# A fused window-attention, linear-attention and routed-expert kernel: zero-padded contraction rows in place of filler matmuls, own PSUM banks for the last expert steps, grouped scatters, and a new order of all steps

## Chip, cores and metric

The kernel runs on one core of a Trainium2 chip. The metric is the device time of one execution in microseconds. The engines are named as in the profile: PE (TensorE), PEld (its weight loads), DVE (VectorE), ACT (ScalarE), POOL (GpSimd), SP (SyncE, which issues DMAs).

## The reference, cut to what matters

The input is 32 images of 56x56 tokens with 64 channels. Three layers follow one another on every token:

```
# layer 0: shifted 7x7 windows, 8 heads of 8, relative position bias, mask; then an MLP with a norm inside
y = ln(x); win = windows(roll(y, -3)); q, k, v = win @ qkv_w.T + qkv_b
x = x + unroll(softmax(q*s @ k.T + bias + mask) @ v @ proj_w.T + proj_b)
h = ln(gelu(ln(x) @ fc1_w.T + fc1_b)); x = x + h @ fc2_w.T + fc2_b
# layer 1a: linear attention over an image, 16 heads of 4
t = ln(x); q, k, v = split(t @ W_qkv.T + b_qkv); kv = einsum(ln(k), ln(v)) / HW
x = x + gelu((q @ kv + t) @ W_proj.T + b_proj) + t
# layer 1b: 8 experts, the best two of each token, weighted by the renormalised softmax
xn = ln(x); x = x + sum_top2(weight_e * (gelu(expert_ln_e(x) @ W1[e] + b1[e]) @ W2[e] + b2[e]))
```

## The kernel before, in words

**Groups and steps.** The tokens are cut into 256 groups of 4 tiles of 98 tokens (two 7x7 windows); an image has 8 groups. Each engine runs a loop over `n`, and in each pass it performs once every short step of the list `ORDER[engine]`. A step's suffix is the group it works on relative to `n`: `s0:+2` computes the scores of group n+2, `fc2:+0` the second MLP matmul of group n, `lp:-10` the linear attention's projection of group n-10 (it needs the sums of the whole image), `rk:-11` the ranks of its tokens among 28 pairs of experts. The order was written out by hand or by a planner; at run time nothing but semaphores ties the engines together. `now`, `before` and `whole` are the waits; `images` runs the list, in steady state from a loop.

**Experts.** Every token is put, by an indirect DMA of POOL, into a queue in DRAM for its pair of experts (`scatter`, four per group). SP reads full tiles of 128 tokens of one pair back (`load_tiles`). There are 271 expert steps of 3 such tiles; step m runs at n = m+26: transposes (`tx`), first matmuls (`ei0` to `ei2`, 8 fp16 matmuls each), gelu on ACT (`h00` to `h23`), second matmuls (`eo0` to `eo2`), weighting on DVE (`yv`, `ya`, `ys`), and three indirect stores of POOL (`so0` to `so2`). A step thus has three tiles, 12 gelus and three stores. Since the groups end at n = 256 and the expert steps at n = 296, the last 40 or so steps run with little or nothing beside them.

**PSUM.** Eight banks: pA serves eight steps of a group in turn (zT, q, z2T, fc11, uT, hT1, oT, proj), pB seven, pO, pP and pS the attention, pK the linear attention, pH the experts' first matmuls, pY both their transposes and their second matmuls. Who may take a bank next is written out in `HANDED`; `handed_on` turns that into a wait.

**Filler matmuls.** `keep_warm` (line 611) issues two fp16 matmuls of 128 rows, 128 columns and 512 moving columns, whose result nobody reads. The PE's list holds eight such steps (fY0, fH0, fS0 to fS2, fB0, fA0, fK0), all at offset -26: they run in every pass that has an expert step, 16 matmuls a pass, and in none of the first 26 passes.

**Contraction rows.** Where a bias is added inside a matmul, the operands have 65 rows: 64 channels and a row of ones (zt, ot, z2t, ut_img, utc on one side, wa, wq2, wp, wf1, wkv, m65 on the other). The router's operands xnt and wrt have 64. `rank` (its first matmul, line 788) and `expert_out` (line 830) contract over a single row, onesf against count or b2pair.

**POOL.** `scatter` waits before each of a group's four DMAs until the one before has landed, `store` likewise before each of its three.

## Time and profile before

| | us |
|---|---|
| median of 3 runs | 9902.23 |
| lowest, highest | 9801.24, 10075.31 |
| the profiled execution, device time | 9946.41 |
| its span, first to last instruction | 9944.6 |
| mean granted TensorE clock in it | 0.821 |

The profile is one execution. Busy time counts an engine's own instructions; idle time in front of an instruction is put down to what released it. A granted clock of 1.00 is 2.4 GHz throughout a stretch, 0.50 is 1.2 GHz throughout. "x" is a count of instructions; an fp32 matmul of the program stands as two matmul instructions. "128*98" in front of a shape are the rows (contraction) and columns that a matmul uses of the array, then comes the moving operand.

### The profile page before, as it was taken

To read this page: it belongs to the slowest core of one execution; us is meant where nothing else is said; L and a number is where in the kernel's file an instruction comes from. 1 tells how busy PE (TensorE), PEld (TensorE's weight loads), DVE (VectorE), ACT (ScalarE), POOL (GpSimd) and SP (SyncE) were. 2 spreads that over 40 slices of the span, in tenths; PEclk is the share of its full clock that TensorE was granted. 3 is DMA by queue.
4 is the path that set the end of the run, shared out by engine and by line. 5 is a ranking of instruction groups with operands and counts; after the bars stand their busy time and mean duration, and the time that the engine had idled before them with its cause. 6 is when DMAs were issued, how large, how long until landed. Compare 5 with 4: busy or idle time off the path is not lost. (4 is left out here: it accounts for less than half of the span.)

```text
span 9944.6 us, 258863 instructions
## 1 busy us (share of the span) xinstructions
PE 9346.8 (94%) x66105; PEld 7341.6 (74%) x66105; DVE 6489.6 (65%) x26878; ACT 5811.1 (58%) x12712; POOL 5304.0 (53%) x7260
## 2 busy tenths in 40 slices
PE   6999999999999999999999999999999999998777
PEld 5777777777777777777777777777777777776544
DVE  4566676577787867677667767677777778673100
ACT  2444566566776756667556656666666667662111
POOL 1344555466665645566555655566665666564311
PEclk8555787699998968899778978899998999886666
DMA  0000000000000000000000000000000000000000
GB/s 22 4 9 9 16 20 17 16 21 21 21 22 20 22 17 19 19 20 21 18 18 19 21 18 19 18 21 20 21 21 19 20 20 22 19 18 21 21 15 9
DMA packets 222232, 181.52 MB, mean 18 GB/s; under 512 B 63338, under 2 KB 193332, under 8 KB 220553
## 3 DMA queue, kind: packets, MB, share of 16 engines
q1 hardware_dynamic: 161128, 84.94, 3.6%
q0 software_dynamic: 59680, 79.82, 2.8%
q8 instruction: 623, 10.21, 0.5%
q14 instruction: 801, 6.55, 0.3%
HBM read 84.61 MB, written 81.62 MB: 17 GB/s over the span
## 5 line engine op out<-in xcount | busy, mean ns | idle before, releaser
L1365 POOL TENSOR_TENSOR sc<-sc,mx 98x392 f32<-98x392 f32 x1024 | 901.6, 881 | 1561.2 <-DVE mx L1013 1495.0
L1606 ACT ACTIVATE ht<-ps,be 128x128 f32<-128x128 f32 x3252 | 1025.2, 364 | 1117.5 <-PE ps L821 534.2
L1428 POOL DMA_INDIRECT slots<-rec,slot x1024 | 1078.3, 1053 | 832.2 <-issue 651.3
L616 PE MATMUL ps<-we_hi,identh 128*128 128x512 f16 x4336 | 1493.1, 448 | 7.7 <-issue 7.3
L1455 POOL DMA_INDIRECT out_y<-ys,row_at x813 | 844.2, 1038 | 738.0 <-issue 297.9
L835 PE MATMUL ps<-we,ht 128*128 x6504 | 1113.3, 326 | 0.0
L835 PEld LDWEIGHTS ps<-we,ht 128*128 128x128 f32 x6504 | 988.6, 233 | 123.7 <-issue 55.0
L651 PE MATMUL ps<-kexp,qbd 128*98 128x392 f32 x2048 | 1028.0, 588 | 5.8 <-DVE sc L1007 3.0
L1007 DVE TENSOR_TENSOR sc<-ps,bias 98x392 f32<-98x392 f32 x1024 | 565.8, 553 | 707.9 <-PE ps L651 676.3
L670 PEld LDWEIGHTS ps<-vexp,pt 98*98 98x98 f32 x8192 | 912.3, 185 | 130.0 <-issue 72.3
L670 PE MATMUL ps<-vexp,pt 98*98 98x36 f32 x8192 | 928.5, 263 | 8.9 <-ACT kexp L1496 8.9
L821 PE MATMUL ps<-xs,we_hi 128*128 128x128 f16 x3252 | 612.7, 240 | 304.1 <-issue 302.0
L1354 POOL TENSOR_TENSOR rs<-ve,cs 98x4 f32<-98x4 f32 x768 | 801.7, 1044 | 20.1
L1481 ACT ACTIVATE pt<-ps 98x392 f32<-98x392 f32 x1024 | 511.8, 500 | 398.9 <-PE ps L670 377.3
L1350 POOL TENSOR_TENSOR ve<-mv,cs 98x4 f32<-98x4 f32 x768 | 218.7, 285 | 940.8 <-DVE mv L967 937.6
L1496 ACT ACTIVATE kexp<-ps,cs 128x196 f32<-128x196 f32 x2048 | 676.7, 462 | 21.2 <-PE ps L635 21.1
L821 PEld LDWEIGHTS ps<-xs,we_hi 128*128 x3252 | 340.8, 105 | 466.4 <-issue 388.8
L659 PEld LDWEIGHTS ps<-cs,pr 98*98 98x98 f32 x4096 | 493.7, 147 | 252.6 <-issue 167.8
L659 PE MATMUL ps<-cs,pr 98*98 98x98 f32 x4096 | 610.5, 279 | 2.4 <-ACT pr L1520 1.7
L616 PEld LDWEIGHTS ps<-we_hi,identh 128*128 128x128 f16 x4336 | 433.9, 117 | 239.4 <-issue 171.2
L821 PE MATMUL ps<-xs,we_lo 128*128 128x128 f16 x3252 | 602.4, 237 | 0.7
L1305 DVE TENSOR_TENSOR yv<-ps,rt 128x384 f32<-128x384 f32 x271 | 149.7, 552 | 682.0 <-PE ps L835 676.8
(233 smaller groups left out, 22351.8 us busy)
## 6 DMA issues: line engine op xcount, KB each, us to landing
rt<-slots SPq DMA_DIRECT2D x813, 66.0 KB
xg<-in_x SPq DMA_DIRECT2D x256, 98.0 KB
slots<-rec,slot POOLq DMA_INDIRECT x1024
out_y<-ys,row_at POOLq DMA_INDIRECT x813
lw<-tile_list SPq DMA_DIRECT2D x271, 0.0 KB
bias<-in_rel SPq DMA_DIRECT2D x1, 1200.5 KB
bias<-in_w SPq DMA_DIRECT2D x2, 512.0 KB
tile_list<-entry SPq DMA_DIRECT2D x64, 0.5 KB
```

Of the source, the lines that this page charges most:

```text
L616: pe.matmul(bank[:, :], identh[:, :], we1[0][:, 0:512], start=True, stop=True)
L651: pe.matmul(pS[0:TOK, 0:HEADS * WA], qbd[:, t, :], kexp[:, t, :], start=True, stop=True)\
L659: last = pe.transpose(pP[0:TOK, cols(h)], pr[:, t, TOK * h:TOK * (h + 1)], ident[0:TOK, 0:TOK])
L670: last = pe.matmul(o[:, :, 2 * h:2 * h + 2, :], pt[:, t % 2, h, :], vexp[:, 2 * t:2 * t + 2, 2 * h:2 * h + 2, :], start=True, stop=True)
L821: last = pe.matmul(pH[:, 128 * (2 * e + h):128 * (2 * e + h + 1)], we1[half][:, bass.ds(pair[e] * HID + 128 * h, 128)], xs[:, q, :], start ...
L835: last = pe.matmul(dst, ht[:, q, 2 * e + h, :], we2[:, bass.ds(chosen[q][e] * 2 + h, 1), :].rearrange("p a c -> p (a c)"), start=False, st ...
L1354: pool.tensor_tensor(rs[L][:, :, :], ve[L][:, :, :], k("minushalf")[0:TOK].unsqueeze(1).to_broadcast([TOK, ve[L].shape[1], GT]), ALU.pow)\
L1365: pool.tensor_tensor(s, s, mx[:, t, :].unsqueeze(2).to_broadcast([TOK, HEADS, WA]), ALU.subtract)\
L1428: pool.indirect_dma_start(slots, bass.IndirectOffsetOnAxis(ap=slot[:, j % 2, t:t + 1], axis=0), rec[:, bass.ts(j % RB, 1), t, :].rearrange ...
L1455: pool.indirect_dma_start(out, bass.IndirectOffsetOnAxis(ap=row_at[:, q:q + 1], axis=0), ys[:, bass.ts(j % 2, 1), q, :].rearrange("p a c - ...
L1496: last = act.activation(kexp[:, :, WA * h:WA * (h + 1)], keys_, ACT.Copy, scale=k("headmask")[:, h:h + 1])
L1606: act.activation(ht[:, q, b, :], pH[:, 128 * b:128 * (b + 1)], ACT.Gelu, bias=be1[:, bass.ds(chosen[q][b // 2] * 2 + b % 2, 1)], scale=1.0 ...
```

## The change

1. **Padded operand rows.** All the 64- and 65-row operands become 128-row ones with zeros below, as do onesf and b2pair; wrt, wa, wp, wf1 and wkv come padded from the host, with the bias row already in them. Four small loads go, nine memsets on DVE in the setup come.
2. **No filler matmuls.** The eight `f..` steps are gone from the PE's list.
3. **Free banks for the last steps.** From expert step 233 (`FIRST_LATE = TOTAL - 23`) on, the transposes go to pA, the first matmuls of the three tiles to pH, pO and pP, the second ones to pY and pS in turn. `groups_done` waits once until the groups are through with these banks.
4. **Scatters and stores in a group.** The waits between the four scatters of a group, and between the three stores of a step, go; one wait for the whole group before stays.
5. **Another order.** All five lists are new but SP's: on PE zT moves from +2 at the head to +3 near the end, v to +1, on DVE st2, mv2, c2 and z2 to +1 and qbd to +3, on ACT sd behind the experts' gelus and just ahead of exp, on POOL the order of sc, so and pw steps.

```diff
-        ut_img = sb("ut_img", [C + 1, TILES * TOK])
+        ut_img = sb("ut_img", [128, TILES * TOK])
...
-        wf1 = sb("wf1", [C + 1, HID])
+        wf1 = sb("wf1", [128, HID])
...
-        load(wf1[0:C, :], fc1w)
-        load(wf1[row, :], fc1b)
+        load(wf1[:, :], fc1w)
...
-            pe="""mix0:+0 fY0:-26 zT:+2 lp:-10 tx:-26 pT0:+1 q:+2 k:+2 fH0:-26 fS0:-26 rk:-11 ei0:-26 mix1:+0 fS1:-26
-                  pT1:+1 fS2:-26 z2T:+0 o0:+1 s0:+2 pT2:+1 o1:+1 fc10:+0 fc11:+0 mix2:+0 ei1:-26 fB0:-26 pT3:+1 xnT:-10
-                  s1:+2 o2:+1 mix3:+0 uT:-1 o3:+1 logit:-10 s2:+2 kv:-1 ei2:-26 mix4:+0 eo0:-26 hT0:+0 hT1:+0 eo1:-26
-                  s3:+2 v:+2 eo2:-26 fA0:-26 oT:+1 fK0:-26 G:-1 proj:+1 fc2:+0""",
...
+            pe="""mix0:+0 lp:-10 k:+2 q:+2 v:+1 rk:-11 tx:-26 z2T:+0 s0:+2 ei0:-26 mix1:+0 pT0:+1 fc10:+0 pT1:+1 mix2:+0
+                  o0:+1 fc11:+0 o1:+1 s1:+2 xnT:-10 uT:-1 mix3:+0 pT2:+1 ei1:-26 logit:-10 pT3:+1 s2:+2 o2:+1 o3:+1 hT0:+0
+                  kv:-1 hT1:+0 ei2:-26 mix4:+0 s3:+2 eo0:-26 oT:+1 fc2:+0 proj:+1 eo1:-26 G:-1 zT:+3 eo2:-26""",
...
+        FIRST_LATE = TOTAL - 23
...
+        def x_bank(m):
+            return pAh if late(m) else pYh
+        def h_bank(m, q):
+            return (pH, pO, pP)[q] if late(m) else pH
+        def y_bank(m):
+            return (pY, pS)[m % 2] if late(m) else pY
...
+            def groups_done():
...
+                if not alone:
+                    alone.append(True)
+                    for signal in ("x1_ready", "hnT_ready", "uT_kept", "o_joined", "pT_ready", "score_bias"):
+                        whole(pe, signal, TOTAL - 1)
...
-                pe.matmul(pB[:, 0:(GT + 1) * NP], onesf[:, :], count[0:1, :].unsqueeze(1).to_broadcast([1, GT + 1, NP]),
+                pe.matmul(pB[:, 0:(GT + 1) * NP], onesf[:, :], count[:, :].unsqueeze(1).to_broadcast([128, GT + 1, NP]),
                           start=True, stop=False)
...
+                if late(m):
+                    groups_done()
+                    if m > FIRST_LATE:
+                        now(pe, "xs_ready", m - 1)
+                else:
+                    handed_on(pe, "tx")
...
-                handed_on(pe, f"ei{q}")
+                if not late(m):
+                    handed_on(pe, f"ei{q}")
+                elif m > FIRST_LATE:
+                    now(pe, "h_ready", m - 1, 4 * q + 3)
...
+            for padded in (zt_, ot, z2t_, ut_img, utc, m65, xnt):
+                dve.memset(padded[C:128], 0.0)
+            dve.memset(onesf[:, :], 0.0)
+            dve.memset(b2pair_[:, :], 0.0)
...
                     whole(pool, "tiles_loaded", g - SCATTER_TO_LOAD - 1)
-                now(pool, "rec_scattered", g, 16 * t - 1, alone="pool")
+                    whole(pool, "rec_scattered", g - 1, alone="pool")
...
-                now(pool, "ys_ready", m)
-                now(pool, "row_ready", m)
-                now(pool, "y_stored", m, 16 * q - 1, alone="pool")
+                if q == 0:
+                    whole(pool, "y_stored", m - 1)
+                    now(pool, "ys_ready", m)
+                    now(pool, "row_ready", m)
+                    pool.sem_inc(held["pool"], 1)
```

## Rows read from the trace of the kernel before

**Rows 1.** The page: the span, and busy time of each engine.
```profile
span 9944.6 us, 258863 instructions
PE 9346.8 (94%) x66105; PEld 7341.6 (74%) x66105; DVE 6489.6 (65%) x26878; ACT 5811.1 (58%) x12712; POOL 5304.0 (53%) x7260
```

**Rows 2.** Busy time by stretch: start, routing, steady, its end, tail, full-speed, half-speed.
```profile
core 0: us, PE busy (x) PEld busy (x) DVE busy (x) ACT busy (x) POOL busy (x), PEclk, DMA share, GB/s
101.00:511.00 410.00, 377.55 (x1823) 299.70 (x1821) 199.91 (x754) 190.32 (x357) 122.96 (x169) 0.60 0.01 4
511.00:1070.00 559.00, 520.88 (x2692) 428.56 (x2690) 353.30 (x1508) 265.50 (x522) 250.29 (x356) 0.55 0.04 9
1070.00:8967.00 7897.00, 7642.45 (x57898) 6062.56 (x57897) 5745.51 (x23867) 5159.39 (x11208) 4669.31 (x6401) 0.87 0.08 19
8967.00:9077.00 110.00, 97.37 (x491) 71.72 (x489) 46.18 (x221) 32.02 (x88) 50.98 (x69) 0.63 0.08 20
9077.00:9944.00 867.00, 666.90 (x2957) 443.62 (x2954) 97.91 (x403) 159.19 (x529) 208.69 (x259) 0.64 0.07 16
2535.00:2781.00 246.00, 234.58 (x2016) 187.06 (x2015) 202.65 (x829) 178.50 (x391) 162.80 (x223) 1.00 0.09 22
1329.00:1375.00 46.00, 46.00 (x220) 36.17 (x220) 23.68 (x102) 20.96 (x44) 19.19 (x26) 0.50 0.05 13
```

**Rows 3.** The same for the experts' transposes (line 802) alone, three to a step.
```profile
1070.00:8967.00 7897.00, 86.33 (x689) 64.92 (x690) 0.87 0.08 19
2535.00:2781.00 246.00, 2.66 (x24) 1.94 (x24) 1.00 0.09 22
```

**Rows 4.** DVE's groups in 9077 to 9908 us: one weighting for each step.
```profile
L1305 DVE TENSOR_TENSOR yv<-ps,rt 128x384 f32<-128x384 f32 x37 | 20.7, 558 | 644.8 <-PE ps L835 644.8
```

**Rows 5.** PE's groups in 2535 to 2781 us: busy, mean ns, idle before.
```profile
L616 PE MATMUL ps<-we_hi,identh 128*128 128x512 f16 x126 | 36.5, 380 | 0.0
...
L696 PE MATMUL ps<-wf,z2t 65*98 65x256 f32 x64 | 15.6, 386 | 0.1
L715 PE MATMUL ps<-wf,hnt 128*98 128x64 f32 x128 | 12.4, 250 | 0.0
...
L684 PE MATMUL ps<-wp,ot 65*98 65x64 f32 x64 | 6.8, 250 | 0.0
...
L635 PE MATMUL ps<-zt,wa 65*64 65x196 f32 x28 | 3.5, 328 | 0.0
```

**Rows 6.** A stretch of the start, 200 to 500 us: all engines, then PE's largest groups.
```profile
200.00:500.00 300.00, 281.92 (x1361) 226.19 (x1359) 152.30 (x579) 143.03 (x271) 92.87 (x130) 0.52 0.01 4
...
L651 PE MATMUL ps<-kexp,qbd 128*98 128x392 f32 x72 | 56.1, 883 | 0.0
...
L696 PE MATMUL ps<-wf,z2t 65*98 65x256 f32 x72 | 33.4, 646 | 0.0
...
L715 PE MATMUL ps<-wf,hnt 128*98 128x64 f32 x129 | 23.4, 374 | 0.0
```

**Rows 7.** PE's timeline around one full-speed filler pair (start us, us).
```profile
2605.13 0.59 PE L616 MATMUL ps<-we_hi,identh 128*128 128x512 f16 x2
2605.56 0.50 PE L659 MATMUL ps<-cs,pr 98*98 98x98 f32 x4
```

**Rows 8.** Waits in 2535 to 2781 us: total us, times, longest.
```profile
POOL sc L1365 <- DVE mx L1013: 26.4, 19, 2.3
...
DVE sc L1007 <- PE ps L651: 9.6, 10, 1.7
```

**Rows 9.** Busy time by stretch for the scores (line 651) alone, eight a group.
```profile
511.00:1070.00 559.00, 88.33 (x120) 25.12 (x120) 0.55 0.04 9
```

**Rows 10.** DVE's timeline in the setup.
```profile
34.01 2.67 DVE L877 MEMSET ut_img<- 1x3136 f32 x1 [0.60 <-issue]
...
48.79 3.15 DVE L931 MEMSET b2pair<- 1x3712 f32 x1 [0.71 <-issue]
```

**Rows 11.** PE's timeline over a step of the tail (start us, us).
```profile
9504.17 0.78 PE L830 MATMUL ps<-b2pair,onesf 1*128 x2
...
9506.78 0.79 PE L830 MATMUL ps<-b2pair,onesf 1*128 x2
...
9514.44 0.53 PE L802 MATMUL ps<-identh,rt 128*128 128x128 f16 x3
...
9516.58 0.24 PE L821 MATMUL ps<-xs,we_hi 128*128 128x128 f16 x1
...
9520.66 0.23 PE L821 MATMUL ps<-xs,we_hi 128*128 128x128 f16 x1 [2.12 <-issue]
```

**Rows 12.** POOL's timeline in the tail: a store behind the one before.
```profile
9517.81 0.98 POOL L1455 DMA_INDIRECT out_y<-ys,row_at  x1 [2.13 <-DMA out_y<-ys,row_at]
```

More of the change, by code:

```diff
@@ L230, in build @@
         pA, pO, pP, pS, pB, pH, pK, pY = ps
-        pYh = pY.ap().bitcast(F16)
+        pYh, pAh = (bank.ap().bitcast(F16) for bank in (pY, pA))
         rec16 = rec.ap().bitcast(F16)
@@ L468, in runs_at @@
                 return n + at == TOTAL
+            if name[0] == "f" and name[1].isupper():
+                return n in range(STEPS + 26)
             if name == "tl":
@@ L605, in transposes @@
                 last.then_inc(S[signal], 1)
-            def keep_warm(name, bank):
-                handed_on(pe, name)
+            alone = []
+            def groups_done():
[3 more added lines that the diff above has]
+                        whole(pe, signal, TOTAL - 1)
+                    pe.wait_ge(mix_dve, 5 * IMAGES)
+                    pe.sem_inc(held["pe"], 1)
+            def keep_warm(name, bank):
+                if late(ran["n"] - 26 if isinstance(ran["n"], int) else None):
+                    groups_done()
+                    bank = pK
+                else:
+                    handed_on(pe, name)
                 for _ in range(2):
@@ L779, in logits @@
                 for t in range(GT):
-                    last = pe.matmul(pB[0:TOK, NE * t:NE * (t + 1)], xnt[0:C, cols(t)], wrt[:, :], start=True, stop=True)
+                    last = pe.matmul(pB[0:TOK, NE * t:NE * (t + 1)], xnt[:, cols(t)], wrt[:, :], start=True, stop=True)
                 last.then_inc(S["logit_psum"], 1)
@@ L1634, in layout @@
     line = lambda a: a.reshape(1, -1)
+    under = lambda w, *b: np.concatenate([w, *b, np.zeros((128 - w.shape[0] - len(b), w.shape[1]), w.dtype)], 0)
     halves = lambda a: a.reshape(2, 128, -1).transpose(1, 0, 2)
```

130 lines of the change are left out of this document (63 added, 67 removed).

## The prediction

> **What bounds the kernel now.** The page comes first. PE is busy 94% of the span, the next engine, DVE, 65% [rows 1]. That is an average over stages, so the second view is the busy time by stretch [rows 2]. In the steady stretch, 1070 to 8967 us, PE is busy 97% and nothing else passes 73%: PE bounds it. It holds 689 transposes, three to an expert step, so 229 steps [rows 3], and a step takes 7897/229 = 34.5 us. In this table the reader is to see the granted clock: 0.87 on average, though PE is hardly ever idle. Two stretches inside it show its levels. In 2535 to 2781 us the clock is 1.00 and eight steps (24 transposes) take 246 us, 30.75 us each. In 1329 to 1375 us it is 0.50, and 220 matmuls take 46 us; at full speed a step has 2016/8 = 252 of them, so a half-speed step takes about 46 x 252/220 = 52.7 us. The 34.5 us lies between: 3.7 us of each step are lost to the clock.
>
> Before 1070 us there are neither experts nor fillers; PE is busy 92 to 94% there and the clock is only 0.60 and 0.55 [rows 2]. After 9077 us only expert steps are left: 37 of them [rows 4] in the 831 us up to the last one's start, 22.5 us each, PE busy 77%, the rest waits for single banks.
>
> The third view is PE's groups at full speed [rows 5]. The fillers (line 616) are its costliest group. Ten other groups have operands of 1, 64 or 65 rows (lines 627, 635, 643, 684, 696, 728, 767, 780, 788, 830), from 15.6 us for line 696 down to 3.5 for line 635.
>
> **The clock, and what padding does to it.** In 200 to 500 us PE is busy 94%, and the clock is 0.52 [rows 6]. In 2535 to 2781 us it is busy 95%, and the clock is 1.00. So being busy doesn't decide. What differs is what PE does: the early stretch has no fillers and no experts, so of its groups only lines 651 and 715 use 128 rows, and everything else has 98 or fewer. I read this as: matmuls that use few rows of the array count for less with whatever grants the clock. Then padding to 128 rows and the fillers are two ways to the same end. Of the matmul time of a full-speed step, the padded groups hold about as much as two times the fillers' (the ten groups sum to 80 us of the stretch, the fillers to 36.5), and it goes from half the array or less to all of it; what is taken away was full. I therefore expect the clock to be at least as high as before.
>
> The Trainium skill has another rule. "TensorE: Matmul & The Clock Gate", Part 1, says that the gate follows how busy the PE has been, and names no rows. By that rule padding is worth nothing and taking the fillers away can only lower the clock; by the trace it is incomplete, since a PE at 94% had 0.52. It would put all the weight on the slower rival below.
>
> Padding itself costs no PE time: line 684 with 65 rows and line 715 with 128 rows, both with 64 moving columns, take 250 ns each [rows 5].
>
> **The change part by part.**
>
> *Fillers.* A pair at full speed starts at 2605.13 and the next group at 2605.56 [rows 7], so 0.215 us each, 16 a step: 3.4 us. PE's work in a full-speed step falls from 234.58/8 = 29.3 to 25.9 us. Now the cover ends: DVE has 202.65/8 = 25.3 us of work in the same step, POOL 20.4 plus the idle issue time in front of its seven indirect DMAs, ACT 22.3 [rows 2]. So PE and DVE are level, and the step can't go below about 26 us. It can't go above the 30.75 us that it has now at full speed unless the new order is worse. At present PE is idle 30.75-29.3 = 1.4 us of a step while DVE has 5.4 us of slack; with no slack left on DVE every wait such as DVE's for scores, 1.2 us a step, and POOL's for maxima, 3.3 us a step [rows 8], hits PE sooner. I take 28.2 us, the middle of 26 and 30.75, because nothing in the rows places it nearer to an end.
>
> *Padding.* The 3.7 us a step lost to the clock stand for a share at half speed of 26% (mean 0.87). I estimate that a fifth of that share is left, since after padding some short stretches of 98-row matmuls and waits remain: 0.6 us. Bounds: 0 and 3.7. Step: 28.8 us; 229 steps: 6595 us.
>
> *Start.* In 200 to 500 us there are 72/8 = 9 groups' scores, a step of 33.3 us [rows 6], so in 101 to 511 some 12 steps; in 511 to 1070 there are 120/8 = 15 of 37.3 us [rows 9]. They are PE-bound at half speed; DVE's work is 200/12 = 17 and 353/15 = 24 us. With full clock they would follow DVE, 20 and 26 us with its gaps; without any gain they stay. These steps lack the experts' 128-row matmuls, so I expect the clock to move up and down and take 26 and 29 us: 410 becomes 320, 559 becomes 435.
>
> *New memsets.* ut_img's took 2.67 us and b2pair's 3.15 [rows 10], both for one partition; the same over 64 or 128 partitions is as long, and the others add about half as much again. That is 9 us in front of everything, on the path: the 101 us ahead of the first stretch become 110. The four loads fewer are taken at nothing, as the wait for the large ones stays.
>
> *Free banks in the tail.* Today the step's transposes start at 9514.44, the first expert matmul at 9516.58, 2.1 us later; the second tile's at 9520.66, held up by the gelus that empty the only bank [rows 11]. A tile's 8 matmuls take 0.95 us, and about 1.0 us of PE's sequencer work lies in front of each tile. With own banks the three tiles end 2.1 + 0.95 + 2 x 1.95 = 7.0 us after the transposes. The second matmuls start every 2.61 us (9504.17 to 9506.78), at half speed, so three take 7.9 us. No fillers between: 15 us. At full clock the latter would be half as long: 11 us. Other limits lie lower: POOL's three stores without a wait take 3 x 1.05 and one landing of 2.1 us [rows 12]. I keep 15, since weight loads and gaps leave the array idle for much of such a step; the range is 11 to 22. 37 x 15 = 555 us. The four steps between 8967 and 9077 still carry the groups' last parts: 110 becomes 96. The stretch behind the last transposes, 36 us, loses two of the stores' waits: 32.
>
> *Scatters in a group.* In steady state POOL isn't the bound and its waits for landings are small; worth nothing there while POOL has its 10 us of slack, which shrinks to 8 at 28.8 us. Without that cover a landing wait of 2.1 us [rows 12] for three of the four scatters would count, 6 us a step, so this edit protects the gain rather than makes one.
>
> *Order.* One activation table load fewer on ACT by the list (sd now stands next to exp), not on the path. The rest of the reordering is what lets PE and DVE come near their 26 us, or doesn't: it is in the 28.2.
>
> **Sum** against the span of 9944.6 us: 110 + 320 + 435 + 6595 + 96 + 555 + 32 = 8143 us. The device time lies 2 us above the span: 8145. The profiled execution is 0.4% above the median of the runs shown; that is within the spread, and I leave 8145.
>
> **Rivals.**
>
> A. *Another engine or the chain takes the place of the fillers.* The fillers stood partly where PE would have waited anyway, so the step stays near its present full-speed length, 31.2 us with a little loss of clock. For it: DVE needs 25.3 us and POOL waits 3.3 us a step for it. Against: PE waits only 1.4 us now. 229 x (31.2-28.8) = 550 us more: 8695. Chance 0.25.
>
> B. *The zeros don't count, slower.* If the clock follows what is multiplied and not how many rows are enabled, or busy time alone, the steady steps look like the start: clock 0.55, nine tenths of the time at half speed. A half-speed step without fillers is 52.7 less 16 fillers at twice 0.215, so 45.8 us, a full-speed one 28.2; mixed: 1/(0.9/45.8 + 0.1/28.2) = 43 us, 9850 us for 229, start as now, 11,600 in all. It decides where a steady step passes (9902-1548)/229 = 36.5 us, which is a share at half speed of 0.6 or a mean clock of 0.70. For it: nothing in the trace has zero rows below an operand. Against: the fillers' own stationary operand is an identity, nearly all zeros, and the transposes' likewise, and stretches full of them are at 1.00. Chance 0.08.
>
> C. *DVE and PE mesh perfectly*, 26.8 us a step: 7687. Chance 0.07. Two engines at 95% or more with semaphores between them speak against it.
>
> D. *Clock and step as forecast*: 0.60; its own range is 7850 to 8450, from 27.5 to 30.1 us a step.
>
> **How the numbers follow.** The likeliest is D: 8145. To hold eight in ten the range takes in D and most of A: 7800 to 8720. It leaves out B, most of C and A's upper end. About 2% is what a measurement of this kernel can tell from no change, as its runs spread by 2.7%. Faster by more than 2%: D, A and C, 0.92. Within 2%: a partial B, 0.02. Slower: 0.06.
>
> **What the profile after would show.** The steady stretch at a clock of 0.93 or more (step "padding"); PE busy about 90% and DVE about 88% there (step "fillers"): if DVE is under 80% and PE has waits of 3 us a step, it is rival A. The start's clock above 0.7. Tail steps of 15 us, first matmuls of the second tile 2 us behind those of the first. The first stretch begins about 9 us later. I am wrong in the main thing if the steady clock is under 0.8, or if the step is under 26 us, which would mean that DVE's busy time itself depends on what runs beside it.

## The result, and the profile after

The changed kernel takes 8790.39 us (median of four runs, 8773.87 to 8800.38). The kernel before took 9988.77 us on the same chip; the ratio is 0.892 with a 95% interval of 0.884 to 0.900. It is faster by over 2%, as forecast, but 645 us slower than the predicted 8145 and 70 us outside the range.

The page of the kernel after: span, and busy time of each engine, beside [rows 1].

```profile
span 8794.7 us, 246765 instructions
...
PE 7712.4 (88%) x61769; PEld 6474.0 (74%) x61769; DVE 6559.0 (75%) x26887; ACT 5510.5 (63%) x12487; POOL 5335.8 (61%) x7260
```

Busy time by stretch of the kernel after, in the columns of [rows 2]: start, routing, steady, its end, tail.

```profile
110.00:422.00 312.00, 257.24 (x1828) 199.25 (x1829) 208.87 (x769) 194.31 (x363) 122.97 (x172) 0.88 0.02 5
422.00:854.00 432.00, 386.51 (x2696) 317.88 (x2695) 355.99 (x1507) 271.42 (x525) 253.73 (x358) 0.75 0.05 12
854.00:8110.00 7256.00, 6521.76 (x54221) 5489.33 (x54220) 5796.40 (x23865) 4845.60 (x10973) 4701.02 (x6399) 0.91 0.08 21
8110.00:8208.00 98.00, 70.71 (x430) 61.08 (x427) 43.97 (x210) 35.11 (x89) 48.30 (x66) 0.57 0.09 22
8208.00:8768.00 560.00, 422.99 (x2292) 362.35 (x2290) 94.75 (x393) 155.47 (x514) 200.74 (x252) 0.50 0.10 25
```

Term by term, predicted and measured: 110 and 110 us ahead of the first stretch, 320 and 312, 435 and 432, **6595 and 7256**, 96 and 98, 555 and 560, 32 and 27. The whole miss, 652 us of span, is in the steady stretch (661). Its 229 steps take 31.69 us each instead of 28.8.

Two parts of that can be told apart. I call a step plain if it isn't the last of an image's eight. In the few plain steps whose granted clock was 1.00 throughout (some 20 of them), the median is 29.76 us: the predicted 28.2 was 1.5 short. The other 1.93 us are lost to the clock; I had 0.6. Those 1.9 us are of two kinds: a plain step dips once, and the last of an image's eight steps takes 38.6 us at a mean clock of 0.74, against means of 29.2 to 31.5 us for the other seven.

Where PE stands idle is in the waits of the kernel after, 2500 to 7000 us, which hold 142 steps (who waited on what; us in total, times, longest):

```profile
POOL sc L1401 <- DVE mx L1049: 750.4, 228, 7.1
...
PE ps L850 <- issue: 195.3, 264, 2.6
...
PE ps L670 <- ACT kexp L1537: 148.0, 115, 1.5
...
PE ps L703 <- ACT ot L1522: 61.0, 124, 0.8
```

These three waits of PE are 1.4, 1.0 and 0.4 us a step (the second is 1.16 with what stands under "issue" there); with the small ones PE is idle 3.2 us of each step. POOL's long wait for DVE costs nothing: DVE itself is busy only 5796/7256 = 80%. PE's timeline shows one of each, three instructions of one step (start us, us, idle before):

```profile
5193.52 0.90 PE L670 MATMUL ps<-kexp,qbd 128*98 128x392 f32 x2 [1.29 <-ACT kexp L1537]
...
5208.72 0.23 PE L850 MATMUL ps<-xs,we_hi 128*128 128x128 f16 x1 [0.93 <-issue]
...
5214.01 0.88 PE L703 MATMUL ps<-wp,ot 128*98 128x64 f32 x8 [0.49 <-ACT ot L1522]
```

"issue" says that nothing the profile knows was waited for. This is line 850, the experts' first matmuls, where PE also loads an entry of the list and works out addresses; e8, e11 and e15 below show that this is what the time goes to. PE's groups of the kernel after in the same stretch (busy us, mean ns, idle before):

```profile
L670 PE MATMUL ps<-kexp,qbd 128*98 128x392 f32 x1136 | 506.8, 528 | 165.2 <-ACT kexp L1537 148.0 <-issue 15.4
...
L850 PE MATMUL ps<-xs,we_hi 128*128 128x128 f16 x1704 | 384.3, 234 | 199.6 <-issue 195.3
L850 PE MATMUL ps<-xs,we_lo 128*128 128x128 f16 x1704 | 374.9, 225 | 0.9
```

The same matmuls in the kernel before, line 821 there, at full speed in 2535 to 2781 us (eight steps):

```profile
L821 PE MATMUL ps<-xs,we_hi 128*128 128x128 f16 x96 | 16.2, 222 | 5.7 <-issue 5.7
...
L821 PE MATMUL ps<-xs,we_lo 128*128 128x128 f16 x96 | 15.8, 218 | 0.1
```

Each matmul is nearly as long as before, at a lower clock, but the idle time in front has doubled, from 0.7 to 1.4 us a step.

### The profile page after: what moved, and what is told of

The parts are those of the page before. It is cut to its first block and busy times, and to the rows that moved or that the text cites. A ratio compares the mean times of both kernels' runs of the same rounds, so it can differ in the third digit from the quotient of the medians.

```text
span 8794.7 us, 246765 instructions
## 1 busy us (share of the span) xinstructions
PE 7712.4 (88%) x61769; PEld 6474.0 (74%) x61769; DVE 6559.0 (75%) x26887; ACT 5510.5 (63%) x12487; POOL 5335.8 (61%) x7260
## 5 line engine op out<-in xcount | busy, mean ns | idle before, releaser
L670 PE MATMUL ps<-kexp,qbd 128*98 128x392 f32 x2048 | 929.1, 536 | 270.9 <-ACT kexp L1537 230.6
L850 PE MATMUL ps<-xs,we_hi 128*128 128x128 f16 x3252 | 753.1, 242 | 445.7 <-issue 436.0
L866 PE MATMUL ps<-we,ht 128*128 x6504 | 976.8, 302 | 0.8 <-issue 0.7
L689 PEld LDWEIGHTS ps<-vexp,pt 98*98 98x98 f32 x8192 | 844.8, 173 | 123.2 <-issue 94.1
L689 PE MATMUL ps<-vexp,pt 98*98 98x36 f32 x8192 | 823.6, 253 | 4.6 <-ACT pt L1522 4.5
L850 PE MATMUL ps<-xs,we_lo 128*128 128x128 f16 x3252 | 736.4, 234 | 1.6
L715 PE MATMUL ps<-wf,z2t 128*98 128x256 f32 x2048 | 713.3, 483 | 0.0
L1537 ACT ACTIVATE kexp<-ps,cs 128x196 f32<-128x196 f32 x2048 | 671.0, 448 | 11.7 <-PE ps L654 11.7
L1049 DVE TENSOR_REDUCE mx<-sc 98x8 f32<-98x392 f32 x1024 | 546.3, 555 | 9.1
L1099 DVE BATCH_NORM_STATS2 st<-hid 98x6 f32<-98x256 f32 x1024 | 382.1, 415 | 224.0 <-ACT hid L1585 190.3
L670 PEld LDWEIGHTS ps<-kexp,qbd 128*98 128x98 f32 x2048 | 270.5, 173 | 349.6 <-issue 348.9
```

The costliest lines, as they stand in the source:

```text
L670: pe.matmul(pS[0:TOK, 0:HEADS * WA], qbd[:, t, :], kexp[:, t, :], start=True, stop=True)\
L689: last = pe.matmul(o[:, :, 2 * h:2 * h + 2, :], pt[:, t % 2, h, :], vexp[:, 2 * t:2 * t + 2, 2 * h:2 * h + 2, :], start=True, stop=True)
L715: last = pe.matmul((pB, pA)[half][0:TOK, (t % 2) * HID:(t % 2 + 1) * HID], z2t_[:, cols(t)], wf1[:, :], start=True, stop=True)
L850: last = pe.matmul(h_bank(m, q)[:, 128 * (2 * e + h):128 * (2 * e + h + 1)], we1[half][:, bass.ds(pair[e] * HID + 128 * h, 128)], xs[:, q, :],
L866: last = pe.matmul(dst, ht[:, q, 2 * e + h, :], we2[:, bass.ds(chosen[q][e] * 2 + h, 1), :].rearrange("p a c -> p (a c)"), start=False, st ...
L1537: last = act.activation(kexp[:, :, WA * h:WA * (h + 1)], keys_, ACT.Copy, scale=k("headmask")[:, h:h + 1])
```

## The experiments

All times are medians; "before" is the kernel before on the same chip, and ratios have their 95% interval. Experiments ran on several chips, on which the kernel before has medians of 9933 to 10028 us, so 1% between two experiments on different chips isn't told. "Full-clock step" is the median over the plain steps whose clock was 1.00 throughout. The kernel after has 29.76 us there, 31.69 us a steady step on average, and a steady clock of 0.91.

### Does padding carry the clock?

**e1_unpadded.** The operands stay in place, but the matmuls read only their 65, 64 or 1 rows:

```diff
-  ... wa[:, C:2 * C], zt_[:, j % 2, w:2 * GT:2, 0, :]
+  ... wa[0:C + 1, C:2 * C], zt_[0:C + 1, j % 2, w:2 * GT:2, 0, :]
```
and so at the nine other matmuls that were padded.

> The changed kernel, but every matmul that was padded reads only its 65, 64 or 1 rows again (fillers stay away, the order stays). Nothing of the result is left out. Theory R (the clock follows how many rows of the array the matmuls enable, zeros included): without the padding the steady stretch falls to a granted clock of 0.5 to 0.65, a steady step takes 42 to 46 us, the whole 11,000 to 12,000 us. Theory B (rows don't matter, only how busy PE is): clock stays near the 0.91 of the changed kernel and the time within 2% of 8790 us.

Measured: 10708 us, ratio 1.073 [1.061, 1.084], slower than before, 38.95 us a step. The steady stretch of this kernel, in the columns of [rows 2]:

```profile
1045.00:9964.00 8919.00, 8672.09 (x54229) 7168.43 (x54229) 5889.46 (x23871) 4922.18 (x10973) 4654.30 (x6401) 0.68 0.07 17
```

PE is busier (97%) than in the kernel after (90%) with the same matmuls, and its clock is 0.68 against 0.91. Rows of zeros raise the clock, so rival B falls. The loss is less than expected, 38.95 us a step and not 42 or more: the clock without padding, 0.68, is above the 0.60 and 0.55 at the start of the kernel before. The tail has the clock 0.50 in both kernels, and there padding shortens work: a tile's second matmuls start 2.62 us apart in e1 and 2.18 in the kernel after (shown below), and the tail takes 597 us against 560.

```profile
10402.64 0.79 PE L861 MATMUL ps<-b2pair,onesf 1*128 x2
...
10405.26 0.79 PE L861 MATMUL ps<-b2pair,onesf 1*128 x2
```

**e3_pad_and_fill.** The kernel after with the lists and the 16 fillers of the kernel before, fillers only from the first expert step on, and no own banks in the tail: padding (with the grouped scatters) alone.

```diff
-        FIRST_LATE = TOTAL - 23
+        FIRST_LATE = 10 ** 6
```
and `ORDER` and `HANDED` of the kernel before.

> The lists and hand-overs of the kernel before with its 16 fillers a step, own banks off, but with padded rows: the padding alone, apart from scatters in a group. Theory R (rows decide the clock): the steady clock rises from 0.87 to 0.98 or more and a steady step becomes 30.7 to 31.0 us, 229 of them 870 us less than before; start and tail about 200 us less at most; 8850 to 9050 us. Theory B (busy time decides): clock stays at 0.87 and the time within 2% of 9900 us.

Measured: 9015.5 us, 0.903 [0.894, 0.913]. Its steady stretch:

```profile
946.00:8107.00 7161.00, 6600.71 (x57886) 5380.91 (x57885) 5764.00 (x23863) 5135.28 (x11207) 4689.42 (x6400) 0.98 0.08 21
```

The step falls from 34.5 to 31.27 us; the full-clock step is 30.49 against 30.75 before. So padding gives back the clock, with 0.8 us a step still lost, and next to nothing of the step at full clock. It isn't that PE has as much to do: its busy time in such a step falls from 29.4 to 28.2 us, half of that in the experts' second matmuls, and its waits grow by 1.1 us, most of it for the gelus (`ht`) in front of them (my own sums over the full-clock steps). The tail takes 775 us, 215 more than with own banks and no fillers.

**e2_old_order.** The lists of the kernel before without their fillers; padding and own banks as after.

```diff
-            pe="""mix0:+0 lp:-10 k:+2 q:+2 v:+1 rk:-11 tx:-26 z2T:+0 s0:+2 ei0:-26 mix1:+0 pT0:+1 fc10:+0 pT1:+1 mix2:+0
+            pe="""mix0:+0 zT:+2 lp:-10 tx:-26 pT0:+1 q:+2 k:+2 rk:-11 ei0:-26 mix1:+0
...
```
and so the rest of the five lists and `HANDED`.

> The changed kernel with the lists of steps and of bank hand-overs of the kernel before, less its fillers: padding, free banks of the last steps and grouped scatters stay. Theory O (the new order is what brought the steady step from 30.75 us at full clock to 29.7): a steady step takes 32.5 to 34 us instead of 31.7, because waits of PE that the fillers had covered now also cost clock; 9000 to 9300 us in all. Theory N (the order is worth nothing, the fillers' time alone was the gain): 8700 to 8850 us, equal to the changed kernel.

Measured: 9311.5 us, 0.932 [0.924, 0.940]; 33.45 us a step at a clock of 0.85, full-clock step 30.27 (two steps only). Beside e3, taking the fillers away under the old order *costs* 2.2 us a step: 0.2 are won at full clock and the rest is lost to the clock. Beside after, the new order is worth 1.8 us a step, 0.5 at full clock and the rest through the clock, and 98 us ahead of the first expert step. The steady step's way from 34.5 to 31.7 us is thus: padding -3.2, fillers taken out +2.2, new order -1.8.

e3 and e2 have the same order, with and without fillers, and show what the fillers covered. PE's groups in 2500 to 7000 us, e3 (144 steps) and then e2 (134 steps):

```profile
L859 PE MATMUL ps<-xs,we_hi 128*128 128x128 f16 x1728 | 296.9, 222 | 137.0 <-issue 135.6
L816 PE MATMUL ps<-count,onesf 128*128 128x140 f32 x288 | 59.3, 288 | 3.0 <-ACT rec L1626 3.0
```

```profile
L859 PE MATMUL ps<-xs,we_hi 128*128 128x128 f16 x1612 | 303.3, 241 | 128.2 <-issue 126.4
L816 PE MATMUL ps<-count,onesf 128*128 128x140 f32 x268 | 71.0, 350 | 75.2 <-ACT rec L1626 72.0 <-remote 1.8 <-issue 1.4
```

Without the fillers PE waits for ACT's `rec` in front of the ranks, 0.5 us a step, and for several other results of ACT and DVE. The idle time in front of the experts' first matmuls (line 859 here) is 0.95 us a step in both: the fillers didn't cover it. In the kernel after, again without fillers, it is 1.4 us, so the growth comes with the new order.

### Fillers in PE's waits

**e4_one_pair**, **e5_three_pairs**, **e6_pairs_in_busy_place.** One pair of filler matmuls in front of s0, where PE waits for the keys' exponentials; two pairs there and one in front of ei2; two pairs in front of eo0, where PE doesn't wait. All only while groups last.

```diff
-  z2T:+0 s0:+2 ei0:-26
+  z2T:+0 fS0:-26 s0:+2 ei0:-26
```
```diff
-  z2T:+0 s0:+2 ei0:-26
+  z2T:+0 fS0:-26 fS1:-26 s0:+2 ei0:-26
...
-  hT1:+0 ei2:-26
+  hT1:+0 fY0:-26 ei2:-26
```
```diff
-  s3:+2 eo0:-26
+  s3:+2 fY0:-26 fY1:-26 eo0:-26
```

> The changed kernel with one filler pair (two fp16 matmuls, 128 rows, 512 columns) a step, on PE right in front of the first scores of a group, where PE waits 1.3 us for ACT's expanded keys; 256 pairs in all, none in the tail. Theory D (the clock drops once in each step because of this thin stretch, and that costs 1 us in a plain step and some 8 in an image's last step): the steady clock rises from 0.91 to 0.97 or more, a steady step falls from 31.7 to 29.8 to 30.3 us, the whole is 8350 to 8500 us. Theory C (a chain through ACT sets the step and the half-speed stretches hide in its waits): the time stays within 1% of 8790 us although the clock rises.

> The changed kernel with three filler pairs a step for the 256 groups: two in front of the first scores (the wait for the expanded keys) and one in front of the third tile's first matmuls, where PE waits 0.9 us. Theory D (the clock drops after the two thin stretches of a step, 2 to 4 and 18 to 20 us into it, which the kernel with one pair still showed): clock 0.98 or more in the steady stretch, a steady step 30.0 to 30.4 us, 8380 to 8520 us in all. Theory C (the fillers now cost as much as the clock gives): 8620 to 8750 us.

> The changed kernel with two filler pairs a step in front of the experts' second matmuls, a place where PE now has no wait: 0.86 us of work at full clock. Theory P (PE is the bound between its own waits): a plain step at full clock grows from 29.8 to 30.5 or 30.6 us. Theory C (a chain through other engines sets the step and PE has slack everywhere): it stays at 29.8 to 30.0 us.

Measured: e4 8657 us, 0.866 [0.858, 0.874]; e5 8441 us, 0.852 [0.845, 0.858]; e6 8639.5 us, 0.872 [0.863, 0.881]. e4 missed its expectation (clock 0.95 and 31.07 us a step): only its image-end step fell, from 38.6 to 31.3 us; its full-clock step is 29.90. The steady stretch of e5, and its groups in 2500 to 7000 us (149 steps):

```profile
863.00:7750.00 6887.00, 6334.24 (x55597) 5151.83 (x55595) 5778.88 (x23866) 4808.19 (x10973) 4736.30 (x6399) 0.99 0.09 22
```

```profile
L673 PE MATMUL ps<-kexp,qbd 128*98 128x392 f32 x1194 | 519.4, 517 | 48.2 <-issue 46.3
...
L853 PE MATMUL ps<-xs,we_hi 128*128 128x128 f16 x1792 | 393.9, 227 | 167.6 <-issue 163.6
```

PE has 1.3 us more to do in each step of e5, its full-clock step is the same (29.80 us), and the clock goes to 0.99: 30.07 us a step. The work fell into waits (at line 670's place 1.16 us have become 0.3) and paid through the clock alone. e6 was meant as the control, with its pairs where PE is busy. Its full-clock step (29.92) is longer by 0.16 us only: the wait for `ot`, 0.44 us, has gone, so even that work was mostly taken from a wait. And it paid too: the steady clock is 0.94, the image-end step 33.0 us, and the time is that of e4 within what two chips can tell. That fillers help only in front of a wait is therefore not shown.

### What holds the full-clock step at 29.8 us?

**e7_no_square_root.** One table load fewer in ACT's step; the deviation of the keys and values is not computed.

```diff
-  act.activation(kvsd[:, :], kvss[:, :], ACT.Sqrt, scale=1.0 / (LD - 1))
+  act.activation(kvsd[:, :], kvss[:, :], ACT.Copy, scale=1.0 / (LD - 1))
```

> The changed kernel without the square root of the linear attention's variances (ACT copies the variance instead, so the keys' and values' norms are wrong); ACT then loads one table less a step, 1.28 us, just in front of its copy for the projection, the exponential, the linear attention's gelu and the expanded keys. Theory A (ACT's chain from there to the expanded keys is what PE waits for): PE's waits for the keys (1.2 us a step) and for the projection's operand (0.4 us) go, a plain step at full clock falls from 29.8 to 28.5 to 28.8 us and the clock rises, 8350 to 8550 us in all. Theory P (another wait takes their place): step within 0.3 us of 29.8 us, time above 8650 us.

**e9_keys_first**, **e10_keys_first_two_pairs.** The keys' matmuls ahead of the projection `lp`, the exponentials ahead of its gelu, the ranks behind s0; the second with two filler pairs.

```diff
-  pe: mix0 lp k q v rk tx z2T s0 ei0      act: tanh lpg ke xc
+  pe: mix0 k lp q v tx z2T s0 rk ei0      act: tanh ke lpg xc
```

> The changed kernel with the wait for the expanded keys taken out by order alone: on PE the keys' matmul stands before the linear attention's projection and the rank step behind the first scores; on ACT the expansion of the keys stands before the linear attention's gelu. Theory K (the 1.2 us wait in front of the first scores is a fixed gap that this order makes, since the keys' expansion queues on ACT behind a gelu that waits for PE): it goes, a plain step at full clock falls from 29.8 to 28.8 to 29.1 us, the dip of the clock early in the step gets rarer; 8350 to 8600 us in all. Theory M (the gelu, now later, holds up the rank step, DVE's first steps and with them the next scores): another wait of 1 us or more appears on PE and the time stays within 1.5% of 8790 us.

> The kernel with the keys first and two filler pairs a step for the 256 groups, one in front of the first scores and one in front of the third tile's first matmuls. Theory K: the steady clock is 0.98 or more, a steady step 29.3 to 29.7 us, 8250 to 8400 us in all, below the 8441 us of the kernel with three pairs. Theory M: 8440 us or more.

Measured: e7 8658 us, 0.874 [0.865, 0.883], full-clock step 29.74 (few such steps). e9 8710 us, 0.879 [0.868, 0.891], 29.74. e10 8473 us, 0.856 [0.845, 0.867], 29.71. PE's waits in 2500 to 7000 us, e7 and then e9:

```profile
PE ps L850 <- issue: 189.1, 277, 2.3
PE ps L670 <- ACT kexp L1537: 169.2, 131, 1.4
...
PE ps L754 <- DVE kvn L1143: 53.6, 129, 0.5
```

```profile
PE ps L850 <- issue: 235.0, 270, 2.6
...
PE ps L807 <- ACT rec L1617: 56.4, 123, 0.9
PE ps L678 <- ACT pt L1522: 37.7, 80, 0.8
```

In e7 the wait for `ot` has gone and one for `kvn` has come. In e9 the wait at the scores has gone, and line 850's has grown from 195 to 235 us while two others came. One table load of ACT and the keys' place are therefore not what sets the step; a wait that is removed comes up elsewhere.

**e8_fixed_experts**, **e11_fixed_experts_on_pe.** PE (and in e8 ACT too) no longer reads from the list which experts a tile is for; the first and second are always taken. Loading the entry and working out the numbers falls away, and the matmuls have constant addresses.

```diff
-  place = pe.value_load(lw[...]) ; pair = [(place // (1 << shift)) % NE ...]
+  chosen[q] = pair = [0, 1, 0]
```

> The changed kernel with experts 0 and 1 for every tile: PE and ACT read no list entries and compute no addresses from them, the matmuls and gelus are as many as before, the values are not. Theory S (PE's sequencer work after a bank comes free costs PE 1.4 us a step in front of the first matmuls of the three tiles): these waits shrink to 0.5 us or less, a plain step at full clock falls to 28.6 to 29.0 us, a tail step from 13.8 to 11.5 to 12 us. Theory A (ACT's chain sets the step): the tail gains as much, but the steady step stays within 0.3 us of 29.8 us and its waits for the keys grow by what the others lose.

> The changed kernel with experts 0 and 1 for every tile on PE alone; ACT still reads the list and computes its bias addresses. Values are not the reference's, the amount of work is. It splits the 2.4 us a step that fixed experts on both engines gave. Theory P (PE's own sequencer is what it was, 1.9 us a step of stretched matmuls and 1.1 us of waits): a plain step at full clock is 27.4 to 27.8 us, about 8050 to 8150 us in all. Theory A (ACT's address work is on the chain, as PE waits for its gelus): 28.6 us or more, above 8350 us.

Measured: e8 8043 us, 0.812 [0.804, 0.820], full-clock step 27.38 us; e11 8084 us, 0.817 [0.802, 0.831], 27.96 us. These are the first to move the full-clock step: 2.4 us for both engines, 1.8 of it PE's. For e8 that is more than was expected (28.6 us or more). Line 850's groups in e8 (line 846 there, 2500 to 7000 us):

```profile
L846 PE MATMUL ps<-xs,we_hi 128*128 128x128 f16 x1857 | 267.3, 224 | 47.8 <-ACT ht L1641 41.6 <-ACT xs L1631 6.1
L846 PE MATMUL ps<-xs,we_lo 128*128 128x128 f16 x1856 | 265.8, 223 | 0.0
```

"issue" is gone, and the busy time per matmul has fallen, 267.3/1857 against 384.3/1704: in the kernel after, the eight matmuls of a tile don't follow each other closely enough to overlap, which a table of busy time can't show as idle.

**e13_early_expert**, **e14_early_expert_two_pairs.** Another order against the same loop: the transposes right behind `lp`, ei0 ahead of s0, and xc ahead of ke on ACT.

```diff
-  pe: lp k q v rk tx z2T s0 ei0      act: lpg ke xc
+  pe: lp tx k q v rk z2T ei0 s0      act: lpg xc ke
```

> The kernel after with one loop shortened: on PE the experts' transposes (tx) stand right behind the linear attention's projection (lp) instead of behind the ranks (rk), and the first tile's first matmuls (ei0) stand ahead of the first scores (s0); on ACT the copy of the transposes (xc) stands ahead of the exponentials of the keys (ke). Nothing is computed differently. What is open: the full-clock step has stayed at 29.7 to 29.9 us whichever wait was filled or taken away. Theory L (one closed loop sets it: projection on PE, gelu and its table load, key exponentials and copy on ACT, then ei0's address work on PE's sequencer and the whole PE stream round to the next projection): ei0's address work now lies in front of the scores' wait, so about 1.1 us of waits go: a full-clock step of 28.4 to 28.9 us, 8450 to 8600 us in all. Theory S (PE's step is its own work plus the sequencer's address work of each tile, about 27.4 + 2.4 us, and the waits only change places): the full-clock step stays at 29.6 to 29.9 us and the time at 8700 to 8800.

> The same order with two pairs of filler matmuls, one ahead of ei0 and one ahead of ei2 (while groups last). Theory L: the full-clock step is 28.5 to 29.1 us and the clock 0.97 or more: 8200 to 8350 us, below the 8441 of the kernel with three pairs. Theory S: full-clock step 29.7 or more, clock 0.98: 8420 to 8500 us. If the fillers cost what they are long, because the wait they stood in has gone: 29.3 to 29.6 us and about 8400.

Measured: e13 8777 us, 0.886 [0.881, 0.891], full-clock step 29.35; e14 8580 us, 0.867 [0.862, 0.872], 29.34. Neither theory's number: 0.4 us came off, and PE's wait at the scores (1.16 us a step) was replaced by one of 1.0 us for DVE's `yv` in front of the transposes. The loss to the clock grew. e14 (30.8 us a step, clock 0.95) is slower than all three of its expectations, and as a kernel worse than e5.

**e15_addresses_in_wait**, **e16_addresses_and_three_pairs.** Nothing is left out. PE's loads and arithmetic for all three tiles stand in one step `ad`, in front of s0, where PE waits anyway; e16 adds the three pairs of e5.

```diff
-  z2T:+0 s0:+2 ei0:-26
+  z2T:+0 ad:-26 s0:+2 ei0:-26
 def expert_in(m, j, q):
-    place = pe.value_load(...); pair = ...; chosen[q] = pair = ...
+    pair = chosen[q]
+def addresses(m, j):
+    for q in range(TILES_PER_STEP):
+        place = pe.value_load(...); pair = ...; chosen[q] = ...
```

> The kernel after, with PE's address work of all three expert tiles (loading the list's entry and working out the two experts and the lane) in one step of the list ahead of the first scores (s0), where PE waits 1.16 us for the keys' exponentials; the first matmuls use the registers later. Nothing is computed differently. Theory S (the address work holds PE up wherever matmuls wait behind it, and it can lie inside a wait): line 850's idle of 1.40 us a step falls below 0.4, the wait at the scores grows from 1.16 to at most 2.6 us, and the full-clock step is 28.6 to 29.3 us; 8550 to 8700 us, as a longer hole in one place may cost clock. Rival (line 850's idle is the matmuls' own register addressing, not the loading): idle before line 850 stays above 1.0 us, the step stays at 29.7 or grows to 30.5: 8800 to 8950 us.

> The same with three pairs of filler matmuls, two ahead of the address step and one ahead of ei2 (while groups last). Theory S: clock 0.98 or more and a full-clock step of 28.9 to 29.4 us: 8250 to 8370 us, below e5's 8441. Rival: full-clock step 29.8 to 30.5, 8440 to 8600 us.

Measured: e15 **8230 us**, 0.823 [0.817, 0.829]; e16 **8209 us**, 0.820 [0.814, 0.826]. Both beat the kernel before and after, and both are below the range expected for them: the step at full clock came out as expected in e15, but the clock rose, where a loss was thought possible. The steady stretch and the tail of e15:

```profile
854.00:7587.00 6733.00, 5970.96 (x54223) 5081.93 (x54223) 5835.45 (x23865) 4806.85 (x10973) 4694.78 (x6399) 0.97 0.09 23
7680.00:8199.00 519.00, 418.22 (x2294) 363.58 (x2291) 95.74 (x394) 155.84 (x514) 200.59 (x252) 0.50 0.11 27
```

PE's groups of e15 in 2500 to 7000 us (152 steps):

```profile
L670 PE MATMUL ps<-kexp,qbd 128*98 128x392 f32 x1223 | 547.7, 530 | 247.3 <-ACT kexp L1541 215.9 <-issue 29.8
...
L846 PE MATMUL ps<-xs,we_hi 128*128 128x128 f16 x1836 | 347.6, 229 | 120.7 <-ACT ht L1651 110.6 <-ACT xs L1639 7.7 <-issue 1.0
```

The full-clock step is 28.71 us, 1.05 less with every instruction still there; line 850's idle for "issue" is gone (1.0 us of 4500), and the wait at the scores has grown by only 0.5 us a step. The rest of the gain, 1.2 us a step, is the clock (0.97; the image-end step is 29.7 us instead of 38.6); why the clock rises, with a PE less busy than in the kernel after (89 against 90%) and a longer wait at the scores, isn't shown. e8's full-clock step is still 1.3 us shorter. Part of that is what the recorded rival named, the matmuls' own register addresses: the third tile's eight first matmuls, which start behind a wait in both kernels, take 1.15 us in e15 and 0.61 in e8, where the addresses are constants (my own means over the full-clock steps). What line 846 still waits for (0.7 us a step) is now ACT's `ht`, which frees the bank. e16 adds 1.3 us of fillers for a clock of 0.99 and is 21 us faster than e15 on the same chip, a quarter of a per cent, while the same pairs were worth some 350 us on the kernel after: e15 has only 0.7 us a step left to win from the clock.

The tail shows it without other work around. PE's timeline in the kernel after: two of a step's second matmuls, then the transposes, the first matmul of each tile of the next step, and its second matmuls:

```profile
8499.46 0.79 PE L861 MATMUL ps<-b2pair,onesf 128*128 x2
...
8501.64 0.74 PE L861 MATMUL ps<-b2pair,onesf 128*128 x2
...
8505.91 0.53 PE L826 MATMUL ps<-identh,rt 128*128 128x128 f16 x3
8508.01 0.29 PE L850 MATMUL ps<-xs,we_hi 128*128 128x128 f16 x1 [1.58 <-issue]
...
8509.99 0.29 PE L850 MATMUL ps<-xs,we_hi 128*128 128x128 f16 x1 [0.79 <-issue]
...
8511.92 0.29 PE L850 MATMUL ps<-xs,we_hi 128*128 128x128 f16 x1 [0.78 <-issue]
...
8513.16 0.79 PE L861 MATMUL ps<-b2pair,onesf 128*128 x2
```

And in e15:

```profile
8047.64 0.53 PE L826 MATMUL ps<-identh,rt 128*128 128x128 f16 x3
8049.09 0.28 PE L846 MATMUL ps<-xs,we_hi 128*128 128x128 f16 x1 [0.92 <-ACT xs L1639]
...
8050.36 0.28 PE L846 MATMUL ps<-xs,we_hi 128*128 128x128 f16 x1
...
8051.62 0.29 PE L846 MATMUL ps<-xs,we_hi 128*128 128x128 f16 x1
...
8052.84 0.79 PE L865 MATMUL ps<-b2pair,onesf 128*128 x2
```

A tile takes 1.27 us instead of 1.98, the whole step 11.7 instead of 13.8: 0.7 us a tile were address work.

### The grouped scatters

**e12_dma_waits_back.** The waits between the four scatters and the three stores are put back.

```diff
-  whole(pool, "rec_scattered", g - 1, alone="pool")
+  now(pool, "rec_scattered", g, 16 * t - 1, alone="pool")
```
and likewise in `store`.

> The changed kernel with the waits between the four scatters of a group and between the three stores of a step put back. Prediction's reading (worth nothing while POOL has slack of 8 us a step; in the tail the stores hide behind 13.8 us steps): steady step within 0.2 us of 31.7 us, 8770 to 8830 us in all. Rival: waits for landings of 2.1 us push the maxima's subtraction and with it the exponential: a steady step of 32.5 us or more, above 8950 us.

Measured: 8739 us, 0.883 [0.867, 0.899], no difference to after that can be told. Its steady step is 31.24 us (expected was within 0.2 of 31.7), its tail 599 us against 560 and its end 30.5 against 27. The loss in the tail lies in its first 16 steps, in which POOL still writes to the queues between the stores: 310 us against 270. In the last 21, where only stores are left, a step takes 13.8 us in both kernels, so the waits between stores cost nothing there. Which of the two kinds of wait costs in the first 16, the run doesn't separate. The first 16 steps, after and then e12:

```profile
8208.00:8478.00 270.00, 200.76 (x1092) 172.27 (x1090) 68.74 (x332) 73.33 (x241) 133.36 (x168) 0.50 0.11 29
8103.00:8413.00 310.00, 199.56 (x1100) 172.45 (x1098) 69.39 (x334) 74.46 (x241) 133.12 (x168) 0.50 0.10 25
```

POOL's timeline in the tail of the kernel after, the three stores of a step, answers [rows 12]:

```profile
8508.62 1.04 POOL L1496 DMA_INDIRECT out_y<-ys,row_at  x1 [7.94 <-DVE ys L1353]
8509.96 0.98 POOL L1496 DMA_INDIRECT out_y<-ys,row_at  x1 [0.30 <-issue]
8511.24 0.98 POOL L1496 DMA_INDIRECT out_y<-ys,row_at  x1 [0.30 <-issue]
```

## Why the prediction was right and wrong

**Fillers, the term that failed.** "3.4 us" of fillers came off the full-clock step as it stood in [rows 5], and the new step was placed at 28.2, "the middle of 26 and 30.75, because nothing in the rows places it nearer to an end". It is 29.76. Adding up only the full-clock plain steps (busy and idle of PE per step, in us, my own sums; e2 has two such steps only):

```
                              before    e3     e2    after    e15
all matmuls: busy              29.35   28.2   25.8   26.1    25.3
             idle               1.3     2.4    4.4    3.75    3.5
experts' first, with idle       2.7     3.0    3.1    4.6     3.1
idle before scores              0.0     0.0    0.0    1.3     1.7
idle before pT, before proj     0.0     0.0    0.0    1.0     1.0
```

PE's busy time fell by 3.2 us, close to the 3.4 that were predicted, but not by the fillers alone: padding took 1.2 of it (e3), and the new order put some back, as the experts' first matmuls follow each other less closely. PE's idle time rose by 2.4. Taking the fillers out by itself, from e3 to e2, made the full-clock step 0.2 us shorter and not 2.5: waits for ACT and DVE came up in their place, 2 us a step. This was rival A's sentence, "the fillers stood partly where PE would have waited anyway", and its signs are what the profile after shows: DVE at 80%, PE's waits 3.2 us a step. That the step of 31.69 is near A's 31.2 is partly luck: A had a longer step with little loss of clock, and it is a shorter one, 29.76, with 1.93 lost. The error was in weighing A: "PE waits only 1.4 us now" was taken as evidence against, but waits that are filled don't show.

A second thing was taken for nothing, the new order's own price. In the old order the second and third tile's first matmuls stand behind long ones (`fc11`, `kv`), start without idle time and take 0.61 us. In the new order the second tile's, behind `pT2`, take 1.04 us, and the third's, behind `hT1`, start after 1.08 us of idle and take 1.16. So 1.5 us more of a step goes to address work than in e2, against what the order gains elsewhere. The experiments show that the order makes this difference; that PE works out addresses while long matmuls still run is my reading of it. That this work exists could have been seen: the prediction itself put "about 1.0 us of PE's sequencer work in front of each tile" into the tail's sum and left it out of the steady step, where it comes three times as well. e8, e11 and e15 show that this is what can be had there: 1.05 us a step by moving it into a wait, 1.8 by leaving it out on PE. Removing the other waits one by one (e7, e9, e13) gave 0.0 to 0.4 us.

Shown is that PE's address work holds the full-clock step up, and that work put into the wait at the scores is free up to about 0.9 us. Not settled is which closed chain through ACT and DVE makes the waits come up elsewhere when one is removed; e13 refuted the one that I had followed back.

**Padding, the mechanism right, its remainder too small.** Padding gives back the clock: e1 and e3 bracket it from both sides. In e3 0.8 us a step stay lost, close to the 0.6 of the prediction (a fifth of 3.7, which the prediction names, would be 0.7). But the sum took that figure for a kernel without fillers, and there 1.93 us are lost, 1.1 of them in the image-end step. The estimate reckoned with "short stretches of 98-row matmuls and waits"; it had no term for what taking the fillers out does to the clock, which e2 and e5 measure: from e3 to e2 the clock falls from 0.98 to 0.85, and with 1.3 us of fillers a step back in the kernel after it rises from 0.91 to 0.99. "Padding itself costs no PE time" was right, and more than that where an operand has one row (e1's tail, e3's busy time). The Trainium skill's rule ("TensorE: Matmul & The Clock Gate", Part 1), that the gate follows how busy PE has been, fits e5 against after (PE busy 92 and 90%). It doesn't fit e1, in which a busier PE with fewer rows has the lower clock, 0.68 against 0.91, nor e15, in which a PE busy 89% has 0.97. Shown is that the rows matter and that 128-row fillers raise the clock; what else decides in these steps stays open.

**Start and routing, right:** 744 us against 755. The clock there is 0.88 and 0.75, "above 0.7".

**Memsets, right:** PE's first transposes of the kernel after start 8.2 us later than before; predicted were 9.

**Own banks, right in the sum, not in the parts.** The tail's 37 steps take 15.1 us on average, with 15 predicted, but unevenly: the first 16 take 16.9 us on average, which wasn't followed up, the last 21 take 13.8. In these the second tile starts 1.98 us behind the first, as computed (1.95), and from the transposes to the end of the three tiles it takes 7.25 us (8505.91 to 8513.16) with 7.0 computed. Half speed was right too, the clock is 0.50 throughout. But the second matmuls start every 2.18 us (8499.46 to 8501.64), not every 2.61 as in [rows 11], so three tiles take 6.5 us and not 7.9. PE isn't idle between them in either kernel. What stretched them in the kernel before is the single row of `b2pair` and `onesf`: e1, without fillers and at the same clock of 0.50, has 2.62 us again. So it is the padding and not the banks that brings these steps below the 15 us of the sum.

**Scatters, right** in the steady stretch, where they are worth nothing (e12). In the tail the edit is worth some 40 us, nearly all in the steps where POOL has both to do; in the last 21 steps, with stores alone, it is worth nothing, and at the very end 3.5 us, for which the prediction had 4.

**The order** was said to be "in the 28.2". It is worth 1.8 us a step against the old lists (e2), so it is the largest gain behind padding, and more through the clock than through the step at full clock. It makes up for most of what taking the fillers out costs under the old lists, 2.2 us a step.

## What to carry to other kernels

Before filler work is priced at its own length, take it out by itself in one run: a wait that is filled doesn't stand in the profile, and here taking out 3.4 us of fillers won 0.2 us of a step at full clock and lost 2.2 us of the average step. When a matmul's address comes from a register, load and compute the registers in one place where the engine waits for data anyway; here that gave some 560 us of 8790 with no instruction removed. Where they can't be moved, look at what an order puts in front of such matmuls: behind long ones the address work didn't show, behind short ones or a wait it did. Pad short contractions with zeros when the array is slowed by its clock and not by its work, and if the clock stays low after that, try a few small full-height matmuls; in this kernel they paid in front of waits and, less for their length, also elsewhere.

## What the runs showed of the hardware that was not expected

- Rows of zeros count for the clock: the same instruction stream has a steady clock of 0.68 with 1, 64 or 65 rows (PE 97% busy) and 0.91 with 128 (90% busy).
- Reading a tile's entry of the list and working out three register values costs PE's sequencer 0.7 us in the tail, with the array idle meanwhile; it shows as "issue" before the matmuls and makes their own busy time look longer (with the idle time 4.6 us a full-clock step, against 3.1 in the old order and 1.8 with constants in e8).
- One 38.6 us step in eight, at a clock of 0.74, went away both with one filler pair in a wait (31.3 us) and with the addresses moved (29.7 us), which is 1.1 us on the average step. What in that step differs wasn't followed up.
- The tail ran at a clock of 0.50 throughout though every expert matmul has 128 rows; PE is busy 76% there. With the fillers and the single banks of e3 it was 0.66, with PE busy 76% as well.
- A pair of matmuls over one row delays what stands behind it more than a pair over 128 rows: at a clock of 0.50 a tile's second matmuls start every 2.62 us in e1 and every 2.18 in the kernel after.
